# The second convolution on skewed rows, and the first one finished by ScalarE and GpSimd

## The reference

```
x = x + newton_schulz_inverse(_gn(x))        # layer 0: 5 iterations of X (2I - W X) on 128 x 128 matrices
x = x + conv3x3(quantised(_gn(x)), w) * s + b # layer 1: int8 values, zero padding, scale and bias
x = x + conv(_gn(x), filter_w[..., :, None] * eye(5))  # layer 2: 5 taps on the diagonal, padding 2
x = x + circular_conv3x3(_gn(x), w)          # layer 3: written with FFTs; equal to a circular 3x3 convolution
```

## Time and profile before

| | |
|---|---|
| median of three runs | 4616.66 us |
| profiled execution, its own time | 4624.59 us |
| its span, first to last instruction | 4622.8 us |
| TensorE busy over the span | 4399.1 us (95%) |
| VectorE / ScalarE / GpSimd busy | 3833.0 / 2251.8 / 2610.2 us |
| mean granted clock of TensorE | 0.986 of full speed |

### The profile page before, as it was taken

The page is one execution under the profiler, slowest core; times in us unless marked ns, Lnnn a source line. Parts: engine busy times, 40 slices in busy tenths (PEclk is TensorE's granted clock), DMA queues, the critical chain, the costliest instruction groups (busy, mean ns, idle before and its releaser), DMA issues. The chain is left out here.

```text
span 4622.8 us, 79863 instructions
## 1 busy us (share of the span) xinstructions
PE 4399.1 (95%) x24265; PEld 3045.4 (66%) x24265; DVE 3833.0 (83%) x8224; ACT 2251.8 (49%) x4551; POOL 2610.2 (56%) x2957
## 2 busy tenths in 40 slices
PE   7999999999999999999999599999999999999998
PEld 6888888888888888888888244444444444444443
DVE  7988898889888988988896687787787778778774
ACT  4766776777677766777776122222222222222221
POOL 7888888888888888888887122222222222222221
PEclk9999999999999999999999799999999999999999
DMA  1111111111111111211111365555556555555554
GB/s 59 61 48 56 56 56 56 56 56 56 56 56 56 56 56 47 63 49 56 56 56 37 84 137 130 130 134 137 125 132 139 127 130 136 132 128 134 137 127 85
DMA packets 333591, 403.08 MB, mean 87 GB/s; under 512 B 23088, under 2 KB 286032, under 8 KB 316880
## 3 DMA queue, kind: packets, MB, share of 16 engines
q1 hardware_dynamic: 284112, 269.46, 18.2%
q10 hardware_dynamic: 49152, 129.59, 16.8%
HBM read 135.22 MB, written 134.22 MB: 58 GB/s over the span
## 5 line engine op out<-in xcount | busy, mean ns | idle before, releaser
L288 POOL TENSOR_TENSOR M<-two,YX 128x256 f32<-128x256 f32 x2560 | 1827.0, 741 | 402.6 <-ACT YX L363 373.4
L758 PE MATMUL bank<-YX,M 128*128 128x256 f32 x8192 | 1948.5, 386 | 40.1 <-issue 40.1
L1147 PE MATMUL bank<-xn,wt 128*128 128x512 f16 (+1 forms) x6912 | 1660.2, 381 | 25.6 <-DVE xn L1003 17.9
L758 PEld LDWEIGHTS bank<-YX,M 128*128 128x128 f32 x8192 | 1504.1, 192 | 227.3 <-issue 44.5
L363 ACT ACTIVATE YX<-bank 128x512 f32<-128x512 f32 x2048 | 1227.5, 599 | 690.8 <-PE bank L758 684.8
L920 POOL TENSOR_TENSOR xn<-F,xn 128x2048 f16<-128x2048 f32 x128 | 487.8, 3811 | 1577.6 <-ACT xn L957 1577.6
L1147 PEld LDWEIGHTS bank<-xn,wt 128*128 128x128 f16 (+1 forms) x6912 | 672.9, 100 | 810.5 <-issue 18.8
L1021 DVE SCALAR_TENSOR_TENSOR x<-bank,wu,x 128x512 f32<-128x512 f32 x512 | 382.2, 746 | 294.7 <-PE bank L1154 283.8
L1154 PE MATMUL bank<-xh,wth 96*128 96x512 f16 (+1 forms) x1792 | 515.4, 380 | 15.3 <-DMA xh<-xn 15.3
L957 ACT ACTIVATE xn<-F 128x2048 f16<-128x2048 f32 x128 | 244.7, 1912 | 475.1 <-DVE F L1077 475.1
L410 DVE BATCH_NORM_STATS2 st<-X 128x6 f32<-128x256 f32 x1024 | 367.8, 410 | 9.6 <-DMA X<-in_x 9.6
(11 more groups left out here) (107 smaller groups left out, 3580.6 us busy)
## 6 DMA issues: line engine op xcount, KB each, us to landing
xh<-xn ACTq DMA_DIRECT2D x768, 131.8 KB, 4.3
X<-in_x SPq DMA_DIRECT2D x64, 1024.0 KB, 4.8
x_scratch<-X SPq DMA_DIRECT2D x64, 1024.0 KB, 5.7
x<-x_scratch SPq DMA_DIRECT2D x64, 1024.0 KB, 6.1
out<-x SPq DMA_DIRECT2D x64, 1024.0 KB, 3.8
xh<-xn ACTq DMA_DIRECT2D x384, 65.9 KB, 2.4
wf<-in_w SPq DMA_DIRECT2D x2, 192.0 KB, 8.5
wf<-in_w SPq DMA_DIRECT2D x1, 320.0 KB, 8.5
```

Of the source, the lines that this page charges most:

```text
L288: nc.gpsimd.tensor_tensor(M[odd][:, at, :], two[:, :].unsqueeze(1).broadcast_to([H, 2, H]), YX[odd][:, at, 0:H], ALU.subtract).then_inc(ma ...
L758: ins = nc.tensor.matmul(banks[u % A_RING][:, 2 * H * m:2 * H * (m + 1)], M[odd][:, 2 * p + m, :], YX[odd][:, 2 * p + m, :], start=True, s ...
L1147: nc.tensor.matmul(bank, wt[l][:, a, k, :], v, start=(k == a == b == 0), stop=False)
```

## The change

Layer 2: five taps on a diagonal become taps in one column if row `r` of each band is shifted left by `r`. SyncE makes that shifted copy `xd` of the high and low part with eight DMAs (`skew`), one for each row `r` of the band, 16 partitions each. The banded matrices of the five shifts then add up to one matrix `wt2` of 128 x 128. The rows that lie in neighbouring bands are taken from `xd` by four DMAs of 32 partitions (`halos2`), which wait for all of `skew`. A chunk has 423 columns, there are five of them, and each takes 5 matmuls: three with `xd` and two with the neighbours' rows. ScalarE takes the result from PSUM (`diagonal_out`), SyncE shifts the rows back into a tile `y` with eight more DMAs of 16 x 16 x 128 numbers (`unskew`), and GpSimd adds `y` to x (`third_x`).

Layer 1: ScalarE takes the chunks from PSUM with scale and bias (`first_out`), and GpSimd adds x (`second_x`). The first pass of `quantise` moves to ScalarE (`first`). Halo DMAs of layer 1 move from ScalarE's to SyncE's queue.

Layer 3 of an image runs one step later than before (`s - 3`), its chunks 0 and 1 before layer 2 and its chunks 2 and 3 after it. The tile `xn2` has one copy, so `upper(2, s)` waits for the skew of image `s - 1`.

```diff
+                    def skew(n, odd):
+                        stand(sp, normed[2], n + 1, w_loaded, 16 * 15)
+                        for r in range(RB):
+                            rows = slice(C * r, C * r + C)
+                            sp.dma_start(xd[odd][rows, :, LEAD + PW - r:LEAD + PW - r + NJ * PW],
+                                         xn2[rows, :, PW:PW + NJ * PW]).then_inc(skewed[odd], 16)
+                    def halos2(n, turn, odd):
+                        stand(sp, skewed[odd], 16 * RB * (turn + 1), w_loaded, 16 * 15)
+                        for part in range(2):
+                            for k, (row, at) in enumerate(((RB - 2, UP), (0, DOWN))):
+                                to = 2 * C * (2 * part + k)
+                                sp.dma_start(xh2[odd][to:to + 2 * C, :],
+                                             xd[odd][C * row:C * row + 2 * C, part,
+                                                     at:at + DIAG * DW]).then_inc(halo[2][odd], 16)
+                    def unskew(n):
+                        stand(sp, evac[2], DIAG * (n + 1), w_loaded, 16 * 15)
+                        for r in range(RB):
+                            rows = slice(C * r, C * r + C)
+                            at = RB - 1 - r
+                            sp.dma_start(y[rows, :, :],
+                                         yd[rows, at:at + NJ * PW].rearrange("p (j w) -> p j w", w=PW)[:, :, 0:H]).then_inc(unskewed, 16)
...
+                        if there(s - 1):                      # SyncE, step
+                            skew(s - 1, 1 - odd)
+                            halos2(s - 1, turns(hb, sb_), 1 - odd)
                         if there(s + 2):
+                            load(s + 2, odd)
+                        if there(s - 1):
+                            unskew(s - 1)
+                        if there(s + 1):
+                            halos1(s + 1, 1 - odd)
+                        if there(s - 3):
+                            store(s - 3, place(h, slot, 3)[1])
...
+                        if there(s - 2):                      # GpSimd, step
+                            third_x(s - 2, place(h, slot, 2)[1])
+                        if there(s):
+                            second_x(s, slot)
+                        if there(s - 2):
+                            lower(3, s - 2, odd)
                         if there(s):
                             lower(2, s, odd)
-                        if there(s - 1):
-                            lower(3, s - 1, 1 - odd)
...
+                    def first_out(n, h, slot, u):             # ScalarE
+                        act.wait_ge(conv_ps[1], BPI * n + u + 1)
+                        nc.scalar.activation(xs[slot][:, 4 * u:4 * u + 4, :],
+                                             chunk_bank(1, u)[:, :].rearrange("p (j w) -> p j w", w=H), ACT.Identity,
+                                             scale=sws[:, 0:1], bias=bst[:, 0:1]).then_inc(evac[1], 1)
+                    def diagonal_out(n, u):
+                        act.wait_ge(conv_ps[2], DIAG * n + u + 1)
+                        nc.scalar.activation(yd[:, DW * u:DW * u + DW], chunk_bank(2, u)[:, 0:DW], ACT.Copy,
+                                             scale=wtop[2]["u"][:, 0:1]).then_inc(evac[2], 1)
...
+                        if there(s - 1):                      # ScalarE, step, after first_out, first and root(3)
+                            for u in (0, 1):
+                                diagonal_out(s - 1, u)
+                        if there(s - 2):
+                            upper(3, s - 2, odd)
+                        if there(s - 1):
+                            for u in (2, 3, 4):
+                                diagonal_out(s - 1, u)
+                        if there(s):
+                            root(2, s)
+                            upper(2, s, odd)                  # waits for the skew of s - 1
                         if there(s - 2):
                             wrap(s - 2, odd)
+                            halos3(s - 2, odd)
...
+                    def conv2(s, odd, turn, u):               # TensorE
+                        bank = chunk_bank(2, u)[:, 0:DW]
+                        at = DOUT + DW * u
+                        if u == 0:
+                            pe.wait_ge(skewed[odd], 16 * RB * (turn + 1))
+                        bank_free(s, 2, u)
+                        for a, b in PRODUCTS:
+                            nc.tensor.matmul(bank, wt2[:, a, :], xd[odd][:, b, at:at + DW], start=a == b == 0, stop=False)
+                        if u == 0:
+                            pe.wait_ge(halo[2][odd], 16 * 4 * (turn + 1))
+                        nc.tensor.matmul(bank, wth2[:, :], xh2[odd][:, DW * u:DW * u + DW], start=False, stop=False)
+                        nc.tensor.matmul(bank, wth2l[:, :], xh2[odd][0:4 * C, DW * u:DW * u + DW], start=False,
+                                         stop=True).then_inc(conv_ps[2], 1)
...
-                        if there(s):
+                        if last:                              # VectorE, step, second half
+                            last_out(s - 3, third, 0)
+                        if old:
+                            normalise(3, s - 2, second)
+                        if now:
+                            deviations(2, s)
+                        if last:
+                            last_out(s - 3, third, 1)
+                        if now:
+                            variance(2, s)
+                        if there(s + 1):
+                            quantise(s + 1, 1 - slot % 2)
+                        if now:
+                            normalise(2, s, slot)
```

517 lines of the change are left out of this document (301 added, 216 removed).

## The result

The changed kernel takes 5236.14 us, the median of four runs (5229.34 to 5256.01); the kernel before, on the same chip, 4616.57 us. The ratio is 1.1348, with a 95% interval from 1.1313 to 1.1382. The forecast was 4850 us with a range of 4520 to 5010. The direction is the forecast one, the loss is 2.7 times the forecast loss, and the time lies above the range, rivals C and D included. The profiled execution has a span of 5254.2 us.

The account below looks back on a forecast made before the run. TensorE's matmuls were taken to bound the kernel at 31.2 us a step. The change's cycle summed to 34.7, taken as 34.5: +211 us over 64 steps and +15 for pipeline ends on 4624.6 gave 4850 us, range 4520 to 5010.

Parts of the forecast that it names:

- C: Rival: TensorE's clock falls to half speed in stage B; cycle 36.5 us, 4979 us; chance 0.15.
- D: Rival: stage B's unskew or GpSimd's adds become the longer way; about 37 us a step, 5010 us; chance 0.08.
- the mechanism: Stage B: a step cannot be shorter than the cycle through skew, `halos2`, layer 2, normalise and low part; 34.5 us.
- Engine sums: Each engine's own work in a stage B step, far under 31.2 us (TensorE 20.0, VectorE 17.4); claimed not to decide.
- the held quantise: VectorE's `quantise` in stage B is held through a port until GpSimd's layer-3 low part ends; waits 2.5 us.
- term 1: The skew in stage B's cycle, eight DMAs of 16 rows in two parts; 10.5 us, between alone and in line.
- the bound from above: Skew with layer-3 halos leaving about 2.4 us earlier, fourteen bursts sharing the engines at 0.88 us; 12.3 us.
- cover: Slack hiding stage B's unskew and adds beside the cycle: 12 us against 16 of skew and `halos2`; 4 us.
- A: Rival, faster: stage B's transfers go at issue pace and quantise is not held; cycle 28.8 us, 4486 us; chance 0.20.
- B: Rival, no change: stage B's transfers at issue pace, with the held quantise; 31.2 us a step, 4640 us; chance 0.12.
- the issue pace: Stage B's DMAs following each other at 0.61 us, so the skew takes 7.6 us and `halos2` 5.1.
- its threshold: Stage B's unskew exceeding some 13 us, which would decide for D.

Follow-up runs that it names:

- both helps: Changed kernel with quantise ahead of layer 2's deviations, layer-1 halos issued before the unskew, and layer-3 halo copies cut to 64 numbers: 4770.31 us.
- the small layer-1 halos: Changed kernel with layer-1 halo copies cut to 64 numbers a partition: 5192.77 us.
- the first and third of those kernels: The early quantise with layer-3 halos waiting for the skew, layer 3's chunks behind layer 2's: 5243.69 us; halos after `halos2` and layer 3's high part: 5068.51 us.
- the early quantise: Changed kernel with VectorE quantising the next image before layer 2's deviations and SyncE issuing layer-1 halos before the unskew: 4943.73 us, ratio 1.0698.
- the small layer-3 halos: Changed kernel with all six layer-3 halo DMAs copying 64 numbers a row instead of 2108: 4881.14 us.

## Why the prediction was right and wrong

- **Right, the mechanism, in two turns of three.** In 36 of 54 turns the step is the cycle through skew, `halos2`, two chunks, both low parts and the normalisation; in the turn shown four of its terms came within 1.2 us. Cutting one term down, the skew's company, moved the step to 34.6 us; the quantise moved it, to 35.7, only with the layer-1 halos moved too. Engine sums had no say, as forecast.
- **Right, the held quantise.** The first pass takes 3.42 us in the turn shown and ends at 4052.91, 1.09 us behind the low part that was under way; its mean is 2828 ns. The extra time is 2.2 us where 2.5 was forecast.
- **Wrong, term 1, the skew: 10.5 us forecast, 16.1 measured in the turn shown and 15.6 in the mean.** This is the step that failed, by its size, and in it the price of what runs beside the skew. The burst itself was priced rightly: 9.5 us alone by the forecast, 9.3 in the mean with both helps. For its company the prediction added 1.0, and 2.8 as the bound from above (12.3). It put the layer-3 halos in line with the skew at 0.88 us each, from a trace in which only one queue sent such bursts, and left the store out. The company costs some 6 us: 4.4 go with the data of the layer-3 halos (11.2 us without them) and about 1.4 with those of the store. With the halos elsewhere the skew took 10.5 and 10.6 us in the turns shown, 11.0 and 10.9 in the mean. From ScalarE's first issue, 2.7 us ahead, to the end of the skew fourteen transfers follow each other every (16.1 + 2.7 - 3.3) / 13 = 1.19 us. A bound worked out from one queue's pace, at a DMA share of 0.59, was no bound for a stretch with a share of 1.00.
- The Trainium skill, "SBUF — State Buffer", section "Door 1: The DMA port swizzle", gave by my estimate 12.4 us for this term. No run bears that estimate out: the skew with the halos elsewhere takes less (10.5 us), and the disturbed one takes more (16.1).
- **Missed, SyncE's list.** It adds 1.65 us to the mean step. Unskew, `halos1`, store and skew stand in one list, and the prediction gave this list cover and no price. The quantise moved alone shows that it is a second way round the step: with the cycle shortened, the skew was issued 8.3 us after its data were ready. The prediction also had the layer-1 halos land before the low part ends; in the turn shown the low part ends at 4023.25 and layer 1's matmul gets its halos at 4025.15.
- **Wrong signs.** TensorE's idle time was to end at layer 2's first chunk. It ends before layer 1, at L1309 (599.5 us, against 84.7 at L1344), a wait that is long but off the cycle, since the small layer-1 halos left the step at 40.0. TensorE is busy for 26 us a step and not 20, at a granted clock of 0.78. The chain names GpSimd and "issue" and hardly SyncE's DMAs (3%).
- **Missed, in the half of layer 1.** The prediction took it for harmless; inside the changed kernel that is true, outside it is not.
- **Rivals.** A and B asked for the issue pace (7.6 us), which no skew kept; B's own terms come to 18.7 behind the transfers and not 18.5, which changes nothing. C: in the changed kernel more clock gave no less time, but it shows where the halos were moved. In the first and third of those kernels layer 2 runs at half speed in every turn, and the term of its first chunks and layer 3's low part is 9.3 us, where it is 8.1 with the early quantise, at full speed. D: its time was reached and passed by another mechanism; the unskew's DMAs land after 4.9 us in the median and are issued in 6.6, under its threshold.

No version tried beats the kernel before. One reason not tested is the DMA engines' own work. Share times step is 32.4 us in the changed kernel (0.79 x 41.0) and 32.1 with the early quantise (0.90 x 35.7). By this estimate no order of the lists gets under the 31.2 us of before, unless packets get shorter once fewer of them run together. It is not what made the step 41.0, since the early quantise does the same work in 35.7. What stays open is what sets the 1.19 us inside the crowded stretch. A full share alone does not: with the small layer-3 halos it is 1.01 in the first 8 us too, and the skew takes 11.3. No run took away the store and the layer-3 halos together.

## What to carry to other kernels

A cycle that runs through a DMA and back makes a pipelined step at least as long as the cycle, whatever the engines' sums say; look for it by asking of each transfer what is waited for until its data return. Price a transfer on such a cycle with the transfers that other queues send at the same moment, not by its pace in a quiet trace. And where engines run strict lists, time an edit in the kernel in which it will live. The same handover of layer 1 lost 400 us in one kernel (180 once GpSimd's adds stood first) and was worth 110 in the other.

## What was unexpected in the hardware

- Issuing a DMA takes 0.59 us at its shortest. In the turn shown it took up to 2.7 us on SyncE's queue, and 4.5 at most over the stage, while ScalarE issued a like burst (six in 8.6 us). With the data of ScalarE's burst taken away it took 0.75 in the median for 1.45. So a burst on one engine can hold another engine's list at its issue, before any landing is waited for.
- `halos2`, the same 132 KB in 32 partitions and one part, lands in 2.4 us with no other queue's burst beside it, at an issue pace of 0.59, where a skew DMA needs 4.4 to 5.5 with the layer-3 halos elsewhere. Beside six layer-3 halos it landed after 6.0 us in the median and up to 7.1.
- The small VectorE product of `dv` with itself (L1209), on 128 x 8 numbers, took 167 ns in the mean before and takes 674 after. In the turn shown one of them runs from 4034.87 to 4036.05 and ends with the last of GpSimd's adds (L1060), which ends at 4036.03. So GpSimd's longer list holds also VectorE work of this size. The instruction ahead of it (L1206, before L1045) was held more often before: 704 ns in the mean then, 334 now.
